# First keys staged in another buffer, weight parts moved to the query phase, and the last block's feed-forward part in halves of 256 tokens

## The reference

```python
# x (4, 2048, 512), ctx (4, 154, 512), 16 heads of 32
def xattn(query, context):
    Q, K, V = query @ Wq.T, context @ Wk.T, context @ Wv.T        # split in 16 heads
    attn = softmax(Q K^T / sqrt(32))
    return (attn V) @ Wo.T
def ffn(x):                                    # x_prev: x shifted by one token, zero first
    xr = mu_r * x + (1 - mu_r) * x_prev
    xk = mu_k * x + (1 - mu_k) * x_prev
    return sigmoid(xr @ W_r.T) * (square(relu(xk @ W_k.T)) @ W_v.T)
x = x + tanh(g_xattn) * xattn(layernorm(x), ctx)
x = x + tanh(g_ffn) * ffn(layernorm(x))
```

## Time and profile before

| | |
|---|---|
| median of 3 runs | 1404.73 us (1402.91 to 1406.04) |
| profiled execution | 1408.19 us, its span 1406.4 us, so 1.8 us lie outside the span |
| instructions | 27977 |
| busy share of the span | PE 97%, DVE 74%, ACT 55%, POOL 42% |
| DMA | 84.07 MB, mean 60 GB/s |

### The profile page before, as it was taken

The page is one execution under the profiler, slowest core; times in us unless marked ns, Lnnn a source line. Parts: engine busy times, 40 slices in busy tenths (PEclk is TensorE's granted clock), DMA queues, the critical chain, the costliest instruction groups (busy, mean ns, idle before and its releaser), DMA issues.

```text
span 1406.4 us, 27977 instructions
## 1 busy us (share of the span) xinstructions
PE 1358.7 (97%) x9436; PEld 992.8 (71%) x9436; DVE 1037.4 (74%) x1928; ACT 777.4 (55%) x1440; POOL 590.5 (42%) x786
## 2 busy tenths in 40 slices
PE   6889999999999999999999999999999999999988
PEld 5656676777767677676777767677776767777667
DVE  5867768687777868778786877868677686877652
ACT  5653746556374655737466473746637465573632
POOL 4333545343453534435353443525344352534333
PEclk8999999999999999999999999999999999999989
DMA  9421011212021121101212111121201112120101
GB/s 298 138 74 46 31 46 60 67 52 58 24 74 45 52 74 52 50 24 67 59 52 74 52 42 33 60 67 52 73 33 51 44 60 67 52 65 18 44 17 44
DMA packets 99179, 84.07 MB, mean 60 GB/s; under 512 B 49488, under 2 KB 64336, under 8 KB 99152
## 3 DMA queue, kind: packets, MB, share of 16 engines
q1 hardware_dynamic: 99152, 83.72, 19.5%
HBM read 57.75 MB, written 20.71 MB: 56 GB/s over the span
## 4 chain that ended last, share of the span: by engine, by line
PE 80%; DVE 8%; ACT 8%; issue 2%; DMA 1%; POOL 1%; SPq 0%; ACTq 0%; DVEq 0%
PE g_bank L1114 45%; PE g_bank L1274 7%; PE o_bank L1221 6%; PE s_bank L1195 4%; PE d_bank L1227 4%; ACT s_bank L663 3%; ACT pq L662 3%; PE s_bank L1171 3%; PE s_bank L1205 2%; DVE buf L815 2%; PE s_bank L1114 2%; PE d_bank L1120 2%; DVE o_bank L955 2%; PE o_bank L1120 1%; DVE d_bank L955 1%
## 5 line engine op out<-in xcount | busy, mean ns | idle before, releaser
L892 DVE TENSOR_TENSOR pq<-s_bank,pq 128x512 f16<-128x512 f32 x320 | 220.4, 689 | 68.9 <-ACT s_bank L663 68.4
L888 DVE TENSOR_REDUCE mm<-s_bank 128x3 f32<-128x462 f32 (+1 forms) x384 | 198.9, 578 | 96.1 <-PE s_bank L1171 96.1
L662 ACT ACTIVATE pq<-s_bank 128x512 f16<-128x512 f32 x320 | 192.2, 601 | 89.3 <-PE s_bank L1199 89.3
L1274 PE MATMUL g_bank<-buf,WkT 128*128 128x512 f32 x744 | 197.0, 412 | 8.6 <-DVE buf L815 6.9
L1114 PE MATMUL g_bank<-xnT,WqT 128*128 128x512 f32 x756 | 196.3, 406 | 0.0
L663 ACT ACTIVATE s_bank<-s_bank 128x512 f32<-128x512 f32 x320 | 194.6, 608 | 0.0
L1114 PE MATMUL g_bank<-WoT,buf 128*128 128x512 f32 x768 | 193.3, 401 | 0.0
L1114 PE MATMUL g_bank<-WrT,buf 128*128 128x512 f32 x744 | 184.2, 397 | 0.0
L490 POOL TENSOR_TENSOR buf<-place,buf 128x512 fp32r<-128x512 f32 x64 | 82.6, 1291 | 235.0 <-ACT buf L568 235.0
L1114 PE MATMUL g_bank<-WvT,buf 128*128 128x512 f32 x708 | 174.4, 395 | 0.0
L1274 PEld LDWEIGHTS g_bank<-buf,WkT 128*128 128x128 f32 x744 | 136.9, 192 | 51.7 <-DVE buf L815 13.8
(11 more groups left out here) (145 smaller groups left out, 2087.9 us busy)
## 6 DMA issues: line engine op xcount, KB each, us to landing
xa<-in_x SPq DMA_DIRECT2D x64, 256.0 KB, 3.2
x<-in_x SPq DMA_DIRECT2D x64, 256.0 KB, 2.7
out<-x SPq DMA_DIRECT2D x48, 256.0 KB, 2.0
place<-x SPq DMA_DIRECT2D x16, 256.0 KB, 2.4
out<-place SPq DMA_DIRECT2D x16, 256.0 KB, 2.0
k_all<-k_scratch SPq DMA_DIRECT2D x15, 256.0 KB, 2.9
k_low<-k_scratch SPq DMA_DIRECT2D x15, 256.0 KB, 2.9
v_main<-v_scratch SPq DMA_DIRECT2D x15, 256.0 KB, 2.8
```

The costliest lines, as they stand in the source:

```text
L662: nc.scalar.activation(pq[:, n, HI, :], bank[:, :], ACT.Exp, scale=SCALE).then_inc(p_hi, 1)
L888: nc.vector.reduce_max(maxima, scores, AX.X).then_inc(reduced, 1)
L892: nc.vector.tensor_tensor(pq[:, n, LO, :], score_bank[5 * g + n][:, :], pq[:, n, HI, :], ALU.subtract).then_inc(p_lo, 1)
L1274: ins = nc.tensor.matmul(bank[c][:, :], WkT2[:, s, e, cols(c)], buf3[:, m, e, :], start=(e, n) == (0, 0), stop=(e, n) == (C - 1, len(PRODU ...
```

## The change

Three edits. **(1)** The first keys are staged in the memory of `x1` (the rows' buffer) in place of `buf4`; ACT's wait for `k_stored` and `k_loaded` goes, and SP waits for them ahead of the first load into `x1`. **(2)** All weight parts are made in the query phase: ACT makes the high parts of Wo, W_k, W_v and W_r three after each query, DVE makes the low parts of W_v between the reductions, POOL those of W_k and W_r between the query's low parts, and POOL takes the low parts of the context's second part from DVE. `fill_group` goes. ACT splits the context's second part ahead of the first values. **(3)** In the last step the filling products keep the order of the loop (r of tile 3 in group 3 ahead of `tail_scores`, v of tile 2 behind it), v of tile 3 follows `values`, and the last block's feed-forward part is done for tokens 0 to 255 and then for tokens 256 to 511: k of a half is 48 matmuls of 256 columns, r and v stay whole tiles. Its queues are written anew for all engines.

```diff
+        first_keys = x1[:, :, :].bitcast(F32R).rearrange("p a n -> p (a n)").rearrange("p (s g n) -> p s g n", s=2, g=G)
...
-            return buf4[:, part, n, 0:2 * P] if item == 0 else k_stage[:, n % 2, part, :]
+            return first_keys[:, part, n, :] if item == 0 else k_stage[:, n % 2, part, :]
...
                     store_first_values()
+                    sp.wait_ge(k_stored, 32)
+                    sp.wait_ge(k_loaded, 16 * K_LOADS)
                     for t in range(TT):
                         load_x1(i, t)
...
+            def ctx_low_later():
+                for m in range(TILES[1]):
+                    parts, tokens = ctx_parts[1], slice(P * m, P * m + P)
+                    pool.wait_ge(ctx_hi, FIRST_TILE[1] + m + 1)
+                    nc.gpsimd.tensor_tensor(parts[:, LO, :, tokens], ctx_loaded_at[1][:, :, tokens], parts[:, HI, :, tokens].bitcast(F32),
+                                            ALU.subtract).then_inc(ctx_lo_pool, 1)
...
-            weight_low(2)
-            for g in range(G):
-                q_low(0, g)
-            weight_low(4)
+            weight_low(units(2))
+            q_low(0, 0)
+            q_low(0, 1)
+            weight_low(units(4)[:2])
+            q_low(0, 2)
+            weight_low(units(4)[2:3])
+            q_low(0, 3)
+            ctx_low_later()
+            weight_low(units(4)[3:])
+            weight_low(units(6))
...
-            late_highs = [*units(3), *units(4)]
+            late_highs = [u for n in (3, 4, 5, 6) for u in units(n)]
             for u in late_highs[:2]:
                 weight_high(u)
-            act.wait_ge(k_stored, 32)
-            act.wait_ge(k_loaded, 16 * K_LOADS)
             for g in range(G):
                 q_split(0, g, False)
-                for u in late_highs[2 * g + 2:2 * g + 4]:
+                for u in late_highs[3 * g + 2:3 * g + 5]:
                     weight_high(u)
-            for m in range(2):
-                kv_high(G + m)
             ctx_high(1)
+            kv_high(G)
+            for u in late_highs[3 * G + 2:]:
+                weight_high(u)
+            kv_high(G + 1)
...
+            norm2(LAST, 0, False)
+            norm2(LAST, 1, False)
+            end_x2_copy(0)
+            end_x2_copy(1)
+            end_k_high(0, 0)
+            norm2(LAST, 2, False)
             for c in range(1, C):
+                end_k_high(0, c)
+            end_x2_copy(2)
+            for c in range(3):
+                end_r_high(0, c)
+            end_x2_copy(3)
+            end_r_high(0, 3)
             for c in range(C):
+                end_relu(0, c)
+            for c in range(C):
+                end_k_high(1, c)
+            end_tanh(0)
+            for c in range(C):
+                end_r_high(1, c)
+                end_k2_high(0, c)
+            end_tanh(1)
+            for c in range(C):
+                end_relu(1, c)
+            for c in range(C):
+                end_k2_high(1, c)
...
+            weight_low(units(3)[:2])
+            reduce_max(0, 0)
+            weight_low(units(3)[2:])
+            reduce_max(0, 1)
+            reduce_max(0, 2)
+            weight_low(units(5)[:1])
+            reduce_max(0, 3)
+            weight_low(units(5)[1:3])
...
+            gated(LAST - 1, TT - 1, V3_END)
+            for t in range(3):
+                residual(LAST, t)
+            end_difference(0)
+            end_k_mix(0, 0)
+            end_difference(1)
+            end_k_mix(0, 1)
+            end_k_low(0, 0)
+            residual(LAST, 3, False)
+            end_k_low(0, 1)
+            end_k_mix(0, 2)
+            end_k_mix(0, 3)
+            end_k_low(0, 2)
+            end_k_low(0, 3)
+            moments2(LAST, 3)
...
-                if ffn and pre:
+                if ffn:
                     ffn_r(i - 1, 3)
-                elif ffn:
-                    ffn_v(i - 1, 2)
...
-                if ffn and pre:
+                if ffn:
                     ffn_v(i - 1, 2)
...
+            def end_k(h, before):
...
+                for e in range(C):
+                    before(e)
+                    pe.wait_ge(xk_lo, halves(h) + e + 1)
+                    for c in range(C):
+                        for n, (s, m) in enumerate(PRODUCTS):
+                            ins = nc.tensor.matmul(K_END[c][:, half(h)], WkT2[:, s, e, cols(c)], xk_end[:, m, e, half(h)],
+                                                   start=(e, n) == (0, 0), stop=(e, n) == (C - 1, len(PRODUCTS) - 1))
...
+            product(V3_END[:, :], lambda s, c: buf1[:, s, c, cols(TT - 1)], lambda m, c: WvT2[:, m, c, :], C).then_inc(v_done, 1)
+            for t in range(2):
+                project(LAST, t, False)
+            project(LAST, 2, False, at(2, lambda: end_x2_transposed(0)))
+            project(LAST, 3, False, at(2, lambda: end_x2_transposed(1)))
+            end_k(0, at(1, lambda: end_x2_transposed(2)))
+            end_x2_transposed(3)
+            end_r(0)
+            end_r(1)
+            end_k(1, lambda e: None)
+            end_r(2)
+            end_r(3)
             for t in range(TT):
+                end_v(t)
```

More of the change, by code:

```diff
@@ L503, in k2_parts, with weight_low @@
                     k2_low(i, c)
-            def weight_low(n):
-                for u in units(n):
+            def ctx_low_later():
[4 more added lines that the diff above has]
+                                            ALU.subtract).then_inc(ctx_lo_pool, 1)
+            def weight_low(some):
+                for u in some:
                     pool.wait_ge(w_hi, u + 1)
@@ L541, in step @@
                 first_column(i)
+                if not pre:
+                    return
                 norm(1, i, 0)
@@ L560, in _ @@
             step(BLOCKS - 1, True, False)
-            k2_parts(BLOCKS - 1)
+            output(LAST - 1, TT - 1)
+            norm(1, LAST, 0)
+            norm(1, LAST, 1)
+            difference(LAST, 0)
+            norm(1, LAST, 2)
+            difference(LAST, 2)
+            norm(1, LAST, 3)
+            difference(LAST, 3)
+            for h in range(2):
+                for c in range(C):
+                    n = halves(h) + c + 1
+                    pool.wait_ge(relu_ready[0], 2 * LAST + C * h + c + 1)
+                    nc.gpsimd.tensor_tensor(k2_end[c], k2_end[c], k2_end[c], ALU.mult).then_inc(k2_ready, 1)
+                    pool.wait_ge(k2_hi, n)
+                    nc.gpsimd.tensor_tensor(buf1[:, LO, c, half(h)], k2_end[c], buf1[:, HI, c, half(h)].bitcast(F32),
+                                            ALU.subtract).then_inc(k2_lo, 1)
             for t in range(TT - 1):
-                output(BLOCKS - 1, t)
+                pool.wait_ge(u_ready, LAST * TT + t + 2)
+                nc.gpsimd.tensor_tensor(x1[:, t, :], th_end[t], x1[:, t, :], ALU.add).then_inc(out_ready, 1)
         @block.scalar
@@ new lines, in end_k_high, with end_r_high, end_relu, end_k2_high @@
+            def end_k_high(h, c):
+                end_high(xk_end, h, c, xk_mixed, xk_hi)
+            def end_r_high(h, c):
+                end_high(xr_end, h, c, xr_mixed, xr_hi)
+            def end_relu(h, c):
+                act.wait_ge(k_done, halves(h) + c + 1)
+                if h:
+                    act.wait_ge(k2_lo, halves(0) + c + 1)
+                nc.scalar.activation(k2_end[c], K_END[c][:, half(h)], ACT.Relu).then_inc(relu_ready[0], 1)
+            def end_k2_high(h, c):
+                act.wait_ge(k2_ready, halves(h) + c + 1)
+                high(buf1[:, HI, c, half(h)], k2_end[c], k2_hi)
@@ L1006, in step @@
                     kv_low_part(G + 1)
-                    ctx_low(1)
+                    weight_low(units(5)[3:])
                 if ffn:
@@ new lines, in end_mix @@
+            def end_mix(h, c, m, column, mixed_ready):
+                dve.wait_ge(diff_ready, LAST * (TT - 1) + (1, 3)[h])
+                dve.wait_ge(diff_last[c // 2], LAST + 1)
+                if c >= 2:
+                    dve.wait_ge((xr_lo, xk_lo)[column], halves(h) + c - 1)
+                elif m > 1:
+                    dve.wait_ge((xk_lo, xr_lo)[column], halves(h if column == 0 else h - 1) + c + 3)
+                nc.vector.scalar_tensor_tensor(MIX_END[c % 2][:, half(h)], diff[:, c, half(h)], mu[:, column, c:c + 1],
+                                               x2[:, c, half(h)], ALU.mult, ALU.add).then_inc(mixed_ready, 1)
@@ new lines, in end_k_mix, with end_r_mix, end_low, end_k_low @@
+            def end_k_mix(h, c):
+                end_mix(h, c, 8 * h + c, 1, xk_mixed)
+            def end_r_mix(h, c):
+                end_mix(h, c, 8 * h + 4 + c, 0, xr_mixed)
+            def end_low(dst, h, c, hi_ready, lo_ready):
+                dve.wait_ge(hi_ready, halves(h) + c + 1)
+                low(dst[:, LO, c, half(h)], MIX_END[c % 2][:, half(h)], dst[:, HI, c, half(h)], lo_ready)
+            def end_k_low(h, c):
+                end_low(xk_end, h, c, xk_hi, xk_lo)
+            def end_r_low(h, c):
```

(11 more changed lines are left out.)

226 lines of the change are left out of this document (120 added, 106 removed).

## The result

The changed kernel took 1394.06 us in the median of four runs (1392.06 to 1395.59), the kernel before, beside it, 1403.93. The ratio is 0.9927, 95% interval 0.9909 to 0.9945: 10 us (0.7%) faster. The profiled execution took 1394.31 us with a span of 1392.6, the one of before 1408.19 and 1406.4.

A forecast was written before the change was run, and what follows sets the result against it. TensorE was taken as the bound, busy 97% of the span, with gains only where it idles or runs at low clock: 0.6 + 5.3 + 8.0 = 13.9 us, giving 1390.8 us; range 1387 to 1397.5.

The forecast's parts named there:

- The stall that takes the place of the one removed: Query phase: TensorE waits 3.6 us ahead of maxima round 1, since ACT waits for W_k's transfer, landing at 31.0.
- Query phase, 0.6 us of gain: Start of the kernel: phase ends at 49.2 instead of 49.8; gain between nothing and 2.1 us.
- Groups 1 and 2, 5.3 us: Step 0: without late weight work each group takes 10.2 us, instead of 12.20 and 13.60; 5.3 us gained.
- Rival D: Step 0: idle time moves instead of going, the 5.3 us are lost, 1396 us; chance 0.10.
- Group 3 stays: Step 0: group 3, 13.02 us at a clock of 0.87, has no weight work in it and doesn't change.
- End, 8.0 us: Last step and last block: 10.4 us of losses go, 1.6 idle and 1.2 matmul cost come; 8.0 taken.
- rival A: Last block: clock falls ahead of k's first half, as after idle times of 2.5 us; 2.2 more, 1393 us; chance 0.12.
- rival B: Last block's k: a 256-column matmul costs a weight load, 0.19 us; 6.1 more, 1396.9 us; chance 0.06.
- rival C: Last block: the half-width mixes are the bound, delaying r and v; 1402.3 us; chance 0.06.
- E: Last block: clock stays low from k's first half to the first v; 19.2 us lost, 1410 us; chance 0.04.
- What is lost now, item by item: End of the kernel before: idle times and low clock, 2.5 + 1.0 + 0.9 + 3.2 + 2.8 = 10.4 us.
- I take the difference to hold for it: Final sum: the profiled execution's 3.5 us above the median of 1404.73 was assumed for the changed kernel too.

The follow-up runs named there:

- the keys alone: Kernel before with only the first keys staged in x1 and ACT's wait for the store gone; 1401.07 us, ratio 0.9967.
- the first new dealing: Changed kernel with ACT's late weight units dealt 2, 4, 3, 3 behind the four queries, not 3, 3, 3, 3; 1391.87 us, ratio 0.9898.
- The order alone: Kernel before with only the last step's filling order of the changed kernel, last block whole, no halves; 1404.28 us, ratio 1.0001.
- The start alone: Kernel before with only keys staged in x1 and all weight parts in the query phase; 1400.36 us, ratio 0.9973.
- the end alone: Kernel before with only the last step's new order and the last block in halves; 1398.99 us, ratio 0.9962.
- The best kernel: Changed kernel with ACT's late weight units dealt 2, 0, 4, 6 and eleven useless matmuls in step 0's two idle times; 1385.77 us, ratio 0.9867.

## Why the prediction was right

The forecast was 1390.8 us, the range 1387.0 to 1397.5, the sign right; measured 1394.06, 3.3 above the forecast. The forecast span, 1392.5, is the profiled one, 1392.6, but by errors that cancel: that agreement is luck. By its steps:

- **The stall that takes the place of the one removed: right.** 3.6 us forecast ahead of round 1, ended by ACT behind W_k's transfer; 3.29, 3.53 and 4.83 in three profiles. That the wait is W_k's is shown by the keys alone and by the first new dealing, which moves one unit in ACT's list and changes nothing else.
- **Query phase, 0.6 us of gain: wrong by its sign.** The transpose of the maxima came at 50.62 and 50.64, 0.8 later than 49.84 and 1.3 to 1.8 later than in the other profiles of that start (48.8 to 49.3). The stall ended at 32.79 and not 32.25, and the slow stretch behind it took 5.30 us for twelve matmuls, where I had nine slow ones in 3.7 and three at full clock; so round 3 came at 41.8 and not 40.3. The rest followed as counted: the context's part 4.9 us behind it, its split, the value unit, the last reduction.
- **Groups 1 and 2, 5.3 us: right.** 25.80 us became 20.71, 5.1 less. Per group 10.36 and 10.35, where 10.2 was counted. Rival D is out. Group 0 was put at no change and lost 0.45 us in this profile and none in the second one of the changed kernel.
- **Group 3 stays: wrong in the profile, right in the code.** It went from 13.02 to 11.33 as the clock didn't fall. Of the six profiles with this part as before, two have 13.0 and four 11.3, so this is chance and no part of the change. That 1.7 us made the profile's sum come out.
- **End, 8.0 us: right in the trace (8.3), 5.3 in the time.** It is 8.3 against an end with the low clock; against the end that kept it (69.98) it is 4.5, and the time lies between. New idle time 1.52 for 1.6, full clock behind it in all eight profiles of this end: rival A is out. A half of k 0.120 to 0.123 us a matmul for 0.126, so 96 cost 11.7 and not 12.1; rival B (0.19) is out. No wait at r or v in the end: rival C is out, and E with it, the clock being 1.00 throughout. By the formula for a lone matmul in the Trainium skill ("TensorE: Matmul & The Clock Gate", section "Back-to-back issue gap") a 256-column one would be 109 ns, an estimate; the trace has 120 with a weight load beside each.
- **What is lost now, item by item: the sum right, the division wrong.** I had put 2.5 + 1.9 us to the fill of the last step by itself. The order alone gave 1.8 in the trace and nothing in the time, for what it fills ahead of `values` it uncovers ahead of k. With the halves it is a gain. The low clock in this list (1.0 + 0.9 + 2.8, 3.7 measured) was counted as always lost, and it isn't.
- **"I take the difference to hold for it": the step that set the error.** The sum was made against a profiled execution 3.5 us above its median, and subtracted from the median. The start alone and the end alone were worth 3.8 and 5.3 us in time, 9.1 together and 10 measured, where the profiles give 13.9. Some 1.7 of the 3.9 us between 13.9 and 10 is group 3's clock in the first profile, and 0.5 to 1.0 its late transpose of the maxima (49.84 where the others have 48.8 to 49.3). The rest is, as far as the runs tell, the low clock at the end: 3.7 us in that profile, and nothing in the profile of the keys alone. How the two share out over all executions stays open.
- **The clock's condition in rival A: a wrong reading of the rows.** "Idle times of 2.5 us and more did that here, one of 1.5 didn't" doesn't hold. In the same profile 1.33 and 1.49 us in step 0 (ahead of 127.56 and 129.62) were followed by 0.50, and the 2.93 us in group 2 that left the clock at 1.00 did lower it in the second profile. That A doesn't come is shown by eight profiles of the new end; the reason given for it isn't shown.

## What to carry to other kernels

When a wait is taken from an in-order engine, list what that engine waits for next and when that lands: here a load that lands at 31 to 33 us took the whole gain of the query phase back, and moving one instruction of ACT's list behind the next query returned 2 to 4 us, dealing the list out anew 6 to 8. Cut the last, unoverlapped stage in two when its first half needs only half of the inputs: k's matmuls cost 0.120 us for 256 columns against 0.228 for 512, and the half that is ready covers the other's preparation. Before a gain read from a profile is subtracted from a median, look at the mean granted clock of the profiled execution beside those of the others (0.990 against 0.993 here), and find the stretches where the clock was low: they may not be low in other executions.

## What the runs showed of the hardware

Between executions of one kernel the time went with the granted clock: in the 29 of the kernel before, 0.990 or 0.991 stood beside spans of 1405.3 to 1406.9 us, and 0.995 or 0.996 beside 1399.8 to 1401.1. The same code took 13.02 or 11.3 us in group 3 and 73.7 or 70.0 us at the end, and 82.95 to 82.99 us a step in the loop every time.

The length of one idle time didn't tell whether the clock fell. Behind 2.52 and 2.79 us it fell in three profiles and not in the fourth; behind 2.9 us in group 2 it fell in the second profile of before and not in the first; behind 1.5 us ahead of k's first half it stayed at 1.00 in all eight; behind 1.33 and 1.49 us with 0.57 us of work between them it fell in all twelve without filling. Nor did a longer one cost more: 4.83 us ahead of round 1 were followed by 12 matmuls in 4.50 us, 3.29 us by 12 in 5.30.

The Trainium skill ("TensorE: Matmul & The Clock Gate", section "HAM oscillation — how this bites in real kernels") tells of the clock falling again and again in a kernel that waits some 3 to 5 us for a transfer between short runs of matmuls. The waits of that length here (3.29 to 4.83 us ahead of round 1) were followed by the low clock too; the falls behind 1.33 and 1.49 us are outside its case. The best kernel runs at a mean of 0.999, with eleven matmuls without use in those two places.
